# Second attention: the causal triangle added by VectorE in place, instead of by identity products on TensorE

## What is computed

```
scores = jnp.einsum('bhqd,bhkd->bhqk', q, k) * scale
scores = jnp.where(causal[None, None], scores, -jnp.inf)
...
scores = scores + head_scales[None, :, None, None] * geo
attn = jax.nn.softmax(scores, axis=-1)
out = jnp.einsum('bhqk,bhkd->bqhd', attn, v).reshape(B, T, C)
```

## Time and profile before

| | |
|---|---|
| timed runs | 1919.35, 1919.41, 1925.64 us; median 1919.41 |
| profiled execution, span from first to last instruction | 1920.6 us |
| TensorE in flight / VectorE / ScalarE / GpSimd | 94% / 74% / 58% / 28% |
| mean granted TensorE clock | 0.956 |
| second attention with its maxima | 1132 to 1550 us |
| router's tail, to the first expert | 1550 to 1614 us |
| experts | 1614 us to the end |

### The profile page before, as it was taken

The page is one execution under the profiler, slowest core; times in us unless marked ns, Lnnn a source line. Parts: engine busy times, 40 slices in busy tenths (PEclk is TensorE's granted clock), DMA queues, the critical chain, the costliest instruction groups (busy, mean ns, idle before and its releaser), DMA issues. The chain is left out here.

```text
span 1920.6 us, 34540 instructions
## 1 busy us (share of the span) xinstructions
PE 1801.7 (94%) x12658; PEld 1172.6 (61%) x12658; DVE 1429.7 (74%) x2814; ACT 1116.8 (58%) x2212; POOL 531.4 (28%) x686
## 2 busy tenths in 40 slices
PE   8989999999999999799999979999999986999995
PEld 4545444444444444488888855556555565999994
DVE  7879999999999999266677655566666544766665
ACT  4645888888888888623232214455364632655555
POOL 5750000333000001142223112212525243444444
PEclk9976999999999999899999978998999998999997
DMA  4883744564334502123354255545566334655555
GB/s 168 286 251 52 123 84 90 135 147 116 82 57 81 85 18 82 34 61 110 110 169 160 88 191 125 144 100 134 154 152 155 89 98 141 154 156 146 142 113 197
DMA packets 146598, 239.16 MB, mean 125 GB/s; under 512 B 25829, under 2 KB 81158, under 8 KB 146448
## 3 DMA queue, kind: packets, MB, share of 16 engines
q1 hardware_dynamic: 113312, 171.48, 36.4%
q0 software_dynamic: 17024, 34.25, 6.8%
q10 hardware_dynamic: 16112, 31.46, 4.6%
HBM read 137.49 MB, written 96.60 MB: 122 GB/s over the span
## 5 line engine op out<-in xcount | busy, mean ns | idle before, releaser
L994 DVE TENSOR_REDUCE b_mx<-b_PM 128x1 f32<-128x512 f32 x1024 | 621.3, 679 | 19.4 <-PE b_PM L848 19.0
L970 ACT ACTIVATE b_probs<-b_PS 128x512 f32<-128x512 f32 x1000 | 523.9, 606 | 70.4 <-PE b_PS L902 55.1
L848 PE MATMUL b_PM<-b_kst,b_qst 48*128 48x512 f32 x888 | 281.4, 431 | 0.0
L2912 ACT ACTIVATE d_probs<-d_PS 128x512 f32<-128x512 f32 (+3 forms) x384 | 166.4, 496 | 191.4 <-PE d_PS L2815 190.8
L902 PE MATMUL b_PS<-b_qst,b_kst 50*128 50x512 f32 x744 | 256.8, 436 | 3.2 <-issue 1.2
L2951 DVE TENSOR_REDUCE d_mx<-d_PM 128x2 f32<-128x1024 f32 (+1 forms) x192 | 179.8, 950 | 102.4 <-PE d_PM L2767 57.4
L902 PEld LDWEIGHTS b_PS<-b_qst,b_kst 50*128 50x128 f32 x744 | 120.5, 184 | 164.2 <-ACT b_probs L970 147.4
L2867 POOL TENSOR_SCALAR_AFFINE_SELECT d_probs<-d_probs 128x128 f32<-128x128 f32 x256 | 75.2, 307 | 273.9 <-ACT d_probs L2912 269.2
L790 POOL CAST b_mhalves<-b_maxima 128x16 fp32r<-128x16 f32 x32 | 6.3, 197 | 505.6 <-DVE b_maxima L1003 505.6
L848 PEld LDWEIGHTS b_PM<-b_kst,b_qst 48*128 48x128 f32 x888 | 142.1, 185 | 5.2
L874 PE MATMUL b_PO<-b_probs,x_v 128*32 128x384 f32 (+2 forms) x2048 | 145.2, 390 | 0.0
(11 more groups left out here) (316 smaller groups left out, 3739.0 us busy)
## 6 DMA issues: line engine op xcount, KB each, us to landing
halves<-a_parts SPq DMA_DIRECT2D x7, 2048.0 KB, 8.7
qk<-c_halves ACTq DMA_DIRECT2D x7, 2048.0 KB
w_w<-L_ffn_fc1T SPq DMA_DIRECT2D x12, 1024.0 KB, 5.0
w_w<-L_ffn_fc2T SPq DMA_DIRECT2D x12, 1024.0 KB, 6.3
b_qst<-halves SPq DMA_DIRECT2D x72, 128.0 KB, 4.4
b_kst<-halves SPq DMA_DIRECT2D x72, 128.0 KB, 7.5
d_qst<-qk SPq DMA_DIRECT2D x36, 256.0 KB, 5.0
d_kst<-qk SPq DMA_DIRECT2D x36, 256.0 KB, 7.0
```

The source lines that it names most:

```text
L848: mm = pe.matmul(PM[n % MBANKS][:], qst[buf][at, p, first:first + P], kst[buf][at, p, kh * BLK:(kh + 1) * BLK], start=True, stop=True)
L970: act.activation(probs[:, s % RING], score_bank(g, s)[:], ACT.Exp).then_inc(exped, 1)
L994: dve.tensor_reduce(mx[:, half, (r * PAIRS0 + p) * TPH + t, kh:kh + 1], PM[n % MBANKS][:], AX.X, ALU.max)\
L2912: act.activation(probs[:, s % RING, 0:w], PS[bank(s)][:, 0:w], ACT.Exp).then_inc(exped, 1)
```

## The change

The two identity products of each diagonal step go, and with them the tile `fixed` and its two copies. TensorE tells VectorE of the step after the second head's product. VectorE adds the triangle (f32, from the constants, the same for both heads) to the last 128 keys of both heads in the PSUM tile, in place, waits for its own addition by a new semaphore, and then takes the maximum as before.

```diff
-        fixed = a.sb("fixed", [P, 2, P], BF16)
-        identb, mask_q = (fixed[:, i] for i in range(2))
...
-        max_scores = a.sem("max_scores")
+        max_scores, max_masked = a.sem("max_scores"), a.sem("max_masked")
...
-                               kst[g % BUFS][0:K, j, kh * BLK:kh * BLK + w], start=True, stop=not diagonal)
+                               kst[g % BUFS][0:K, j, kh * BLK:kh * BLK + w], start=True, stop=True)
                 if j == G1 - 1:
-                    if diagonal:
-                        for i in range(G1):
-                            mm = pe.matmul(PM[n % MTILES][:, i, w - P:w], identb, mask_q, start=False, stop=True)
                     mm.then_inc(max_scores, 1)
...
-            for i, at in enumerate((C_IDENT, C_MASK_Q)):
-                dve.tensor_copy(fixed[:, i], const[:, at:at + P])
+            mask_q = const[:, C_MASK_Q:C_MASK_Q + P].unsqueeze(1).to_broadcast([P, G1, P])
...
-                n = entry["max", g, t] % MTILES
-                dve.tensor_reduce(mx[:, :, qt, kh], PM[n][:, :, 0:keys(qt, kh)], AX.X, ALU.max).then_inc(max_taken[n], 1)
+                n, w = entry["max", g, t] % MTILES, keys(qt, kh)
+                if kh == qt // TPK:
+                    near = PM[n][:, :, w - P:w]
+                    dve.tensor_tensor(near, near, mask_q, ALU.add).then_inc(max_masked, 1)
+                    dve.wait_ge(max_masked, g * TPB + qt + 1)
+                dve.tensor_reduce(mx[:, :, qt, kh], PM[n][:, :, 0:w], AX.X, ALU.max).then_inc(max_taken[n], 1)
```

More of the change, by code:

```diff
@@ L2761, in max_product @@
                 w = keys(qt, kh)
-                diagonal = kh == qt // TPK
                 n = entry["max", g, t]
```

## The result

The changed kernel took 1933.79 us (median, 1926.70 to 1937.62), against 1919.38 us for the kernel before beside it: a ratio of 1.0074 (1.0055 to 1.0094). A second set of six runs, beside 27 of before, gave 1.0087 (1.0066 to 1.0108). The change costs 13 and 15 us by the difference of the means, 14 and 17 by the ratios. The forecast was 3 us, and the time lies above its range.

The account below looks back on a forecast made before the run. The prediction took TensorE to set the pace, with VectorE's release of the two PM tiles deciding. Its terms, -9.6 + 3.0 + 6.9 + 1.2 + 1.5 = +3.0 us on 1919.4, gave 1922.4 us, range 1909 to 1932.

Parts of the forecast that it names:

- The work: Diagonal steps: 87 product pairs saving TensorE 0.11 us each, 9.6 us gained; 128 VectorE additions of 428 ns.
- Quiet groups: Slots without router work: a new 0.2 us wait at query tile 6 in 15 groups, 3.0 us lost.
- Before the slots: Start of the attention, where VectorE and TensorE take turns, with six steps of group 1: 1.5 us lost.
- Router passes: Three passes in the loop: longer waits for maxima queued behind router work, 3 x (1.1 + 0.46 + 0.7) = 6.9 us lost.
- the product behind query tile 7: In each router pass, the product waiting for query tile 7's maximum, reached late by VectorE: 0.46 us more wait.
- the dense stretch: Densest VectorE part of each router pass: a wait growing by 0.46 to 0.92 us, 0.7 taken.
- Rival 2: Router stretches: VectorE becomes the bound, 20 us lost in place of 6.9, about 1935 us; chance 0.17.
- Keys: Where the loop waits for key loads, earlier gains are waited away: four groups at 0.3 us, 1.2 us lost.
- rival 3: TensorE's clock: two more half-clock stretches as in the first router pass, +13 us, about 1935 us; chance 0.07.

Follow-up runs that it names:

- e1: Kernel before with neither identity products nor additions, the triangle left out of the maxima altogether; ratio 0.9985 to the kernel before.
- e2: Kernel before with its identity products kept and the VectorE additions put in too; ratio 1.0081 to the kernel before.
- f3: Kernel before with additions in the 24 diagonal steps of slots 56 to 67 of each router pass, identity products elsewhere; ratio 1.0069 to the kernel before.
- e5: Changed kernel with 72 dummy identity products put where TensorE was seen waiting; ratio 1.0053 to the kernel before.

## Why the prediction was wrong, point by point

- **The work.** 128 additions at 0.423 us (0.428 forecast), each maximum 0.03 us behind its addition, 0.11 to 0.13 us saved per pair, not 0.22. Right, and e1 gives 9.8 us at an equal clock for the forecast 9.6. But beside the additions the products' removal brings only 5.8 us (e2 against the changed kernel): the sum added two terms that are not independent, and some 4 us are lost by it.
- **Quiet groups.** 0.57 to 0.60 us faster each, 0.4 to 0.5 forecast. Nearly right: no product waits at query tile 6 in the quiet group shown, where a new wait of 0.2 us was forecast.
- **Before the slots.** The first turning came 16.8 us behind the first product of the maxima, 15.4 before: 1.4 us, with 1.0 forecast. Group 1's six steps behind it took 0.3 us more (0.5).
- **Router passes: too small by some 2 us.** The projections waited 5.0 us more in all (3.3 forecast), the product behind query tile 7 0.73 us more (0.46), the dense stretch 1.0 us more in one place and 0.4 in the other (0.7). f3's 24 steps leave the dense stretch out; it gives 6.7 us net at an equal clock, where 3 x (1.1 + 0.46) less 24 x 0.11 = 2.0 was forecast. The waits above account for some 4.6 of it. Rival 2 said 20 us; no run shows that.
- **Keys: open.** I took 1.2 us for four groups. The waits grew by 4.0 us in one profiled execution and shrank by 2.1 in the other. In both, the wait for group 4's keys grew from 1.5 us to 3.8 and 4.0: the gain until there was waited away, and the load, issued earlier, was in use no earlier. The short loads take the whole cost at an equal clock away (5.6 to -0.4 us), so keys or their traffic have a part in it; how large the term is by itself stays open.
- **The clock: the step that failed.** The sum has no term for it: it was made at the clock of the kernel before, and a lower one stood only in rival 3, with a chance of 0.07. The changed kernel spends 21 to 24 us more at 1.2 GHz, worth 9 to 10 us at 0.41 each, more than all other errors together (2.6 us: 5.6 at an equal clock for the forecast 3.0). Rival 3 was right in size and time (1935 us), not in place: it looked for two more stretches of 12 to 13 us in the router passes. In the profiled executions the groups behind the three passes have 10.9 and 2.2 us at 1.2 GHz in all, against 9.6 before, and the groups with neither a pass nor its end went from 24 us to 33 and 37. I set the rival aside because the second pass in the trace of before had the same waits and kept its clock. But that was one execution: in the trace of before, as in the one after, the same kind of group runs at 1.00 in one pass and at 0.85 or 0.83 in another. A change that makes waits longer and takes work out changes how often that happens, and one execution does not show how often. Why the clock falls at one place and not at another stays open.

The Trainium skill, "TensorE: Matmul & The Clock Gate", section "A second HAM failure mode: psum-queue depth-cycling", was the rule that spoke for rival 3: short idle times of TensorE between groups may make the clock swing. The runs here agree with it in direction: products out (e1), 13 us more at 1.2 GHz; longer waits added (e2), 6 us, within the scatter; both, 24 us; the waits filled (e5), 27 us less.

## What to carry to other kernels

Work taken from an engine that sets the pace is worth its length only while the clock stays; where waits already exist, forecast a change with two terms, one at an equal clock and one for the clock, and read the latter from the mean clock of many runs, not from one trace. An instruction added to a chain that two engines hand back and forth can cost more than its length where that chain stands behind other work (one projection's wait grew by 0.67 us for an addition of 0.42): 24 of 128 additions cost 12.3 us by themselves. Two edits that meet in such a chain should not be added up as if each were alone. Such a change is best made step by step, as the choice per slot here allows, and its early part cost nothing.

## What the hardware showed unexpectedly

- Useless products in TensorE's waits brought the changed kernel's half-clock time down from 189 to 162 us, and its ratio from 1.0087 to 1.0053. The first is clear of the noise; the second, a difference of two sessions, is at its edge.
- Issuing a group's key loads 1.15 us earlier did not bring them into use earlier (1208.92 and 1208.87). Putting the loads some 10 us earlier in the queue made the kernel 37 us slower, with 13.3 us of waits for the small row copies behind them and 11.9 us more waits for maxima.
- The same kind of group of slots, with all but equal work, took 27.44 us at 2.4 GHz throughout and 31.96 us with 10.9 us at 1.2 GHz: 0.41 us for each microsecond, as over whole runs. The same pair in the trace of before gives 0.50.
